# Layer 1 of a two-layer conv and scan kernel: another order of the steps, and y taken from PSUM by VectorE with xs times D in the same instruction

## The reference

```
x     = silu(depthwise_conv_5x5(x) + conv_b);  xs = x.reshape(B, C, L)
x_dbl = einsum('kd,bdl->bkl', x_proj_w, xs);   dts, Bs, Cs = x_dbl[:, :R], x_dbl[:, R:R+N], x_dbl[:, R+N:]
delta = softplus(einsum('dr,brl->bdl', dt_w, dts) + dt_b)
log_dA = maximum(delta * A, log(EPS));  P = exp(cumsum(log_dA, -1))
hs    = P * cumsum(delta * Bs * xs / maximum(P, EPS), -1)
y     = einsum('bdnl,bnl->bdl', hs, Cs) + xs * Ds
```

## Time and profile before

| | us |
|---|---|
| three runs | 4332.36, 4338.97, 4346.80; median 4338.97 |
| the profiled execution | 4340.87, of which the span in the trace is 4339.1 |
| layer 1 begins | about 1987 |
| one group inside the loop, from gate to gate | about 300 |
| the last group | about 249 |

### The profile page before, as it was taken

The page is one execution under the profiler, slowest core; times in us unless marked ns, Lnnn a source line. Parts: engine busy times, 40 slices in busy tenths (PEclk is TensorE's granted clock), DMA queues, the critical chain, the costliest instruction groups (busy, mean ns, idle before and its releaser), DMA issues.

```text
span 4339.1 us, 74865 instructions
## 1 busy us (share of the span) xinstructions
PE 3840.0 (88%) x22806; PEld 2793.4 (64%) x22806; DVE 3258.9 (75%) x5219; ACT 2790.3 (64%) x4796; POOL 2263.5 (52%) x1928
## 2 busy tenths in 40 slices
PE   6999999999999999887888889888888888898877
PEld 6787878888787878675555545545545555455432
DVE  3767666676767675605988978879879889789899
ACT  1545455454636363657887877878778778778775
POOL 0323223232323242405776867767768677677787
PEclk9999999999999999987997988979979979889877
DMA  7565555556464644373423324424324334243100
GB/s 233 146 186 150 174 161 160 174 147 183 135 196 124 212 123 142 80 184 82 109 71 92 103 57 106 115 51 109 98 61 108 79 81 109 61 108 92 37 20 22
DMA packets 314879, 507.44 MB, mean 117 GB/s; under 512 B 190000, under 2 KB 255248, under 8 KB 314144
## 3 DMA queue, kind: packets, MB, share of 16 engines
q1 hardware_dynamic: 314432, 502.08, 42.3%
HBM read 424.94 MB, written 77.07 MB: 116 GB/s over the span
## 4 chain that ended last, share of the span: by engine, by line
PE 22%; DVE 12%; issue 9%; ACT 7%; POOL 5%; DMA 1%; DVEq 1%; ACTq 0%; POOLq 0%; SPq 0%
PE ps_front L1313 6%; PE ps_y L1386 5%; DVE ps_q L1080 5%; DVE h L1107 5%; PE ps_front L1306 3%; PE ps_prep L1335 2%; POOL u L1000 2%; PE ps_y L1383 2%; POOL h L1011 2%; PE ps_front L1326 1%; PE ps_bc L1356 1%; ACT d_a L1201 1%; DMA out_dram<-y 1%; ACT d_a L1195 1%; ACT y L1221 1%
## 5 line engine op out<-in xcount | busy, mean ns | idle before, releaser
L1011 POOL TENSOR_TENSOR h<-h,c_rows 128x448 f32<-128x448 f32 x672 | 766.7, 1141 | 366.1 <-DVE ps_q L1114 194.6
L522 ACT ACTIVATE act_h<-ps_up,b 128x448 f32<-128x448 f32 x672 | 408.9, 635 | 778.5 <-PE ps_up L640 778.3
L1000 POOL TENSOR_TENSOR u<-dxs,b_rows 128x448 f32<-128x448 f32 x672 | 767.0, 1141 | 48.0 <-ACT b_rows L1209 42.3
L1386 PE MATMUL ps_y<-h,ident 128*128 128x448 f32 x1344 | 733.2, 633 | 35.0 <-POOL h L1011 25.4
L319 POOL TENSOR_TENSOR h_low<-act_h,h_high 128x448 fp32r<-128x448 f32 x224 | 287.7, 1284 | 900.6 <-ACT h_high L527 900.6
L1080 DVE TENSOR_TENSOR_SCAN ps_q<-d_a,q_last,ps_q 128x448 f32<-128x448 f32 x576 | 659.6, 1145 | 13.2 <-ACT d_a L1201 13.2
L1107 DVE TENSOR_TENSOR_SCAN h<-d_a,ps_q 128x448 f32<-128x448 f32 x576 | 648.3, 1126 | 6.5 <-issue 6.2
L1313 PEld LDWEIGHTS ps_front<-win,taps 120*112 120x112 f32 x4608 | 538.4, 188 | 139.8 <-issue 136.4
L613 PE MATMUL ps_stage<-win,taps 124*112 124x112 f32 x6144 | 607.2, 260 | 2.7 <-DVE w_low L366 2.7
L613 PEld LDWEIGHTS ps_stage<-win,taps 124*112 124x112 f32 x6144 | 607.0, 178 | 3.3 <-DVE w_low L366 2.8
L1313 PE MATMUL ps_front<-win,taps 120*112 120x112 f32 x4608 | 550.8, 273 | 7.5 <-ACT win L1151 3.7
(11 more groups left out here) (93 smaller groups left out, 7156.2 us busy)
## 6 DMA issues: line engine op xcount, KB each, us to landing
taps<-in_t_dram SPq DMA_DIRECT2D x192, 896.0 KB, 4.9
taps<-in_t_dram SPq DMA_DIRECT2D x192, 672.0 KB, 4.9
xres<-in_x_dram SPq DMA_DIRECT2D x224, 168.0 KB, 2.5
x_dram<-x1o SPq DMA_DIRECT2D x224, 168.0 KB, 2.0
x1pad<-x_dram SPq DMA_DIRECT2D x96, 392.0 KB, 8.1
out_dram<-y SPq DMA_DIRECT2D x168, 224.0 KB
xpad<-in_x_dram SPq DMA_DIRECT2D x29, 1176.0 KB, 10.4
conv<-in_x_dram SPq DMA_DIRECT2D x3, 1176.0 KB, 14.9
```

The source lines that it names most:

```text
L522: nc.scalar.activation(act_h[u % 2][:, t, :], ps_up[t][:, 0:BT], ACT.Gelu, bias=b1[:, t:t + 1]).then_inc(gelu_done, 1)
L1000: nc.gpsimd.tensor_tensor(u[s % U_SLOTS][:, :], dxs[:, t, :], b_rows[n][:, :], ALU.mult).then_inc(u_done, 1)
L1011: nc.gpsimd.tensor_tensor(h[s % H_SLOTS][:, :], h[s % H_SLOTS][:, :], c_rows[n][:, :], ALU.mult).then_inc(hc_done, 1)
L1386: nc.tensor.matmul(ps_y[:, 0:BT], ident[:, :], h[s % H_SLOTS][:, :], start=False, stop=(n == N - 1)).then_inc(y_added, 1)
```

## The change

1. `skip` and its product are gone. The first `add_y` of a run starts the accumulation.
2. `keep_y` moves from ScalarE to VectorE: one instruction reads `ps_y`, adds `xs` times `ds_col`, and writes `y`. It stands in the step in which TensorE's last add of the run stands (s = 5, 9, ... in place of ScalarE's 6, 10, ...), right behind `gate`. The last run of a group is taken in step 1 of the next. `silus` now waits for `y_kept`, since VectorE reads `xs` so late.
3. The tables change: `DELTA_AT = (4, 5, 8)`, `Z_AT = (5, 6, 9)`, `SUM_AT = (8, 9)` with the third tile at j = 0 of the band itself, `DXS_AT = (9, 11)` with the third at j = 1.
4. The front begins a step later, ends two steps earlier (three convs of the last block have both halves in one step), and the bursts stand at s = 0 (6 pieces), 41 (3), 63 (7) and 70 (5).
5. Within a step TensorE now does the pieces of the next band ahead of the front piece; ScalarE does the late softplus ahead of `keep_b`, and most front pieces at the step's end.
6. VectorE's first group is written out ahead of the loop, which now has six turns on that engine.

```diff
-        DELTA_AT = (3, 5, 7)
-        Z_AT = (4, 6, 8)
-        SUM_AT = (7, 9, 11)
-        DXS_AT = (8, 10, 11)
+        DELTA_AT = (4, 5, 8)
+        Z_AT = (5, 6, 9)
+        SUM_AT, LAST_SUM_AT = (8, 9), 0
+        DXS_AT, LAST_DXS_AT = (9, 11), 1
...
+            def keep_y(g, r):
+                b, t = r // TILES, r % TILES
+                dve.wait_ge(y_added, g * S + (r + 1) * N + H_SLOTS)
+                dve.wait_ge(y_stored, (g * RUNS + r + 1) * 16)
+                nc.vector.scalar_tensor_tensor(y[:, :], xs[:, t, b * BT:(b + 1) * BT], ds_col[:, t:t + 1],
+                                               ps_y[:, 0:BT], ALU.mult, ALU.add).then_inc(y_kept, 1)
...
                     gate(g, s)
+                    if s > N and (s - N - 1) % N == 0:
+                        keep_y(g, (s - N - 1) // N)
+                    if s == 1 and not first:
+                        keep_y(g - 1, RUNS - 1)
+                    if j == LAST_SUM_AT:
+                        sum_delta(g, b, TILES - 1)
                     if (more or b + 1 < BANDS) and j in SUM_AT:
                         sum_delta(f, fb, SUM_AT.index(j))
...
+                    act.wait_ge(y_kept, (f - 1) * RUNS + b * TILES + t + 1 + Y_BASE)
                     nc.scalar.activation(xs[:, t, b * BT:(b + 1) * BT], bank[i][:, 0:BT], ACT.Silu,
                                          bias=conv_bias[:, t:t + 1]).then_inc(front_kept, 1)
...
                 if n == 0:
-                    pe.wait_ge(y_kept, g * RUNS + r + 1)
-                    nc.tensor.matmul(ps_y[:, 0:BT], skip[:, t, :], xs[:, t, b * BT:(b + 1) * BT],
-                                     start=True, stop=False)
+                    pe.wait_ge(y_kept, g * RUNS + r + Y_BASE)
                 pe.wait_ge(hc_done, g * S + s + 1 + N)
                 nc.tensor.matmul(ps_y[:, 0:BT], ident[:, :], h[s % H_SLOTS][:, :],
-                                 start=False, stop=(n == N - 1)).then_inc(y_added, 1)
+                                 start=(n == 0), stop=(n == N - 1)).then_inc(y_added, 1)
```

More of the change, by code:

```diff
@@ L815, in layer1 @@
         KEPT = (BANDS - 1) * STEPS
+        Y_BASE = RUNS + 1
         CONVS = CB // CQ
@@ L822, in layer1, with place @@
         units, schedule, backs = [], [[] for _ in range(S)], [[] for _ in range(S)]
-        def place(step, unit):
-            for piece in range(HALVES if unit[0] == "conv" else 1):
-                schedule[step + piece].append((len(units), piece))
+        def place(step, unit, at_once=False):
+            i, count = len(units), HALVES if unit[0] == "conv" else 1
             units.append(unit)
+            for piece in range(count):
+                schedule[step].append((i, piece))
+                if piece + 1 == count or not at_once:
+                    step += 1
+            return step
         def place_backs(step, runs):
@@ L1129, in group @@
                     scan_h(g, s)
-            for t in range(TILES):
+            for t in range(TILES - 1):
                 sum_delta(0, 0, t, True)
-            if last:
-                with dve.Fori(0, last) as g:
-                    group(g, True)
+            assert last > 1
+            group(0, True, True)
+            with dve.Fori(1, last) as g:
+                group(g, True)
             group(last, False)
+            keep_y(last, RUNS - 1)
         @block.scalar
@@ L1392, in group @@
                     f, fb = next_band(g, b)
[L1393 to L1397 removed]
+                    prepare = more or b + 1 < BANDS
+                    burst = backs[s] if more or s == 0 else ()
+                    starts = [i for i, piece in schedule[s] if piece == 0] if more else ()
+                    early = [i for i in starts if units[i][0] == "turn"] if not burst else ()
+                    for i in early:
+                        front_waits(g + 1, i)
                     if s >= Y_LAG:
                         add_y(g, s - Y_LAG)
[L1400 removed]
+                    if burst and starts:
                         for i in burst:
[L1402 to L1403 removed]
+                            back(g + 1, i)
+                    for i in starts:
+                        if i not in early:
                             front_waits(g + 1, i)
@@ L1406, in group @@
                         spread_c(g, b, SPREAD_C_NOW[j])
+                    for t in range(TILES):
+                        if prepare and j == PROJECT_AT[t]:
+                            project(f, fb, t)
+                    if prepare and j in DELTA_AT:
+                        delta_rows(f, fb, DELTA_AT.index(j))
+                    if prepare and j in SPREAD_B_AT:
+                        spread_b(f, fb, SPREAD_B_AT.index(j))
+                    if prepare and j in SPREAD_C_AT:
+                        spread_c(f, fb, SPREAD_C_AT.index(j))
+                    if burst and not starts:
+                        for i in burst:
+                            back(g if s == 0 else g + 1, i)
                     if more:
```

103 lines of the change are left out of this document (40 added, 63 removed).

## The result

| | before | changed |
|---|---|---|
| median of the runs | 4342.08 us | 4984.73 us |
| lowest and highest | 4332.36, 4346.8 | 4980.59, 4989.76 |
| profiled execution, its span | 4339.1 us | 4988.0 us |

The ratio is 1.1484, with a 95% interval of 1.146 to 1.1508: 643 us slower. The forecast was slower too, but 4690 us, and even its upper end, 4868, was too low.

A forecast was written before the change was run, and what follows sets the result against it. VectorE was taken as the bound. To 4340.9 us were added 91 (instruction), 212 (j = 9), 61 (j = 1), 163 (bursts), -284 (old waits), 113 (clock) and -4 (small things), +352: 4690 us, own range 4490 to 4870, chance 0.75.

The forecast's parts named there:

- the first row of VectorE's waits: Sign on VectorE: a new first row, y waiting for TensorE's add, 168 instances, about 4 us in every band at j = 9.
- VectorE's instruction: On VectorE: 168 new y instructions at 0.54 us each on its path, +91 us (91 to 109).
- The waits of before: VectorE's old waits, for softplus, `u` and smaller things, all go: -284 us (bounds 200 and 284).
- j = 9: VectorE's y at band step 9 waits for TensorE's last add: 4.3 us in 42 bands, 2.2 in 14, +212 us.
- j = 1: VectorE's y at band step 1 waits 1.7 us for TensorE in five bands of seven groups: +61 us.
- The ring: Steps j = 7 to 9: VectorE's `delta`, ScalarE's clip and `b_rows`, TensorE's spread to last add, VectorE's y; 7.2 us against 2.85.
- The bursts: At steps 63, 70 and 0, y waits behind TensorE's bursts: 22.5 us in seven groups, 5 in the last, +163 us.
- The store: At step 63's burst, the store, which had made a copy wait 1.91 us there, was counted in y's 9 us wait.
- The clock: TensorE's clock falls during waits: 1.7 us in 42 rings, 6 us at seven group starts, +113 us (0 to 290).
- A: Rival: only VectorE's list counts, old waits stay about as they are, 4341 + 91 = 4432 us; chance 0.12.
- C: Rival: TensorE, relieved of 390 us, stays ahead and each last add ends before gate plus 0.54; 4228 us; chance 0.09.

The follow-up runs named there:

- store_early: The changed kernel with SyncE's store of y ahead of the loads of its step and two steps earlier: 4888.42 us.
- late3_store: The changed kernel with y two steps later on VectorE and SyncE's store ahead of the loads, ScalarE's list unchanged: 4365.48 us.
- y_alone: The kernel before in its order, with y on VectorE, no diagonal product or copy, and three back pieces moved to the next group's first step: 4709.48 us.
- The halves: Against the kernel before: the changed order with y made the old way, 4365.78 us; the old order with y on VectorE, 4709.48 us.

## Why the prediction was half right

The sign, the first row of VectorE's waits and the mechanism were right; the size was not. Point by point, by its own terms:

*VectorE's instruction*, +91: it was 99. It is 0.678 us long, not 0.61, and 0.59 on the path.

*The waits of before*, -284: right to a few us. Softplus has vanished from the rows and `u` is down to 2.2.

The waits in front of y were forecast as 212 + 61 + 163 + 113 = 549, and were 844. With the clock's shares put where the prediction had them, and the waits summed up from the timeline over all eight groups:

| the y of | forecast | measured |
|---|---|---|
| j = 9, 42 bands with front work | 181 + 71 = 252 | 313.3 |
| j = 9, 14 bands without | 31 | 62.7 |
| j = 1, five bands of seven groups | 61 | 168.0 |
| s = 5, 65 and 73 of seven groups | 157 + 42 = 200 | 271.4 |
| elsewhere in the last group | 5 | 22.4 |
| elsewhere | 0 | 6.3 |

The 295 us of difference are the whole error (4985 - 4690).

*j = 9.* The ring was right, link by link, and opening it gave 198 us. Where nothing else came in, the size was right too: 4.3 + 1.7 = 6.0 us forecast, 5.9 and 6.3 at s = 21 and 33. That is partly luck, since the 1.7 was no more than a third of a bound. The rest has other causes: TensorE comes late out of the burst at s = 45 (8.7), the store holds y at s = 57 (9.0), and at s = 9 (7.5) and 69 (7.2) more of the ring runs at the low clock. The 14 bands without front work were given no clock at all; at s = 81 both adds of the ring take 1.86 us. There y waits 5.0 us, and 4.6 in the last group, not 2.2.

*j = 1* is the largest miss, and here the step failed: it was counted at full clock, and the clock term had nothing for it. Measured were 2.9 to 5.1 us, and 8.6 at s = 61, where the store adds to it, in place of 1.75. At s = 25 VectorE was ready 13.4 us behind the y of j = 9, as counted (13.3), but TensorE's last add ended at 18.4 and not at 15.0: the wait at j = 9 had come back to TensorE as a wait of 2.67 us, and behind it the turn, the add and the projections ran at the low clock (1.71, 1.86 and 3.35 us, where the count had 1.8 for the projections).

*The bursts*, 22.5 us a group and 6 for the clock: the y of s = 5, 65 and 73 waited 15.6, 13.6 and 9.0 us, 38.2 together, where I had 6.5, 9 and 7. At s = 65 it is the store; without it (store_early) 7.4. The largest miss is s = 5. TensorE there, in the fourth group, whose first gate is at 3146.1:
```profile
3162.97 1.70 PE L1322 MATMUL ps_front<-ident,x1pad 32*120 32x32 f32 x15
3164.60 1.86 PE L1400 MATMUL ps_y<-h,ident 128*128 128x448 f32 x2
...
3175.63 1.86 PE L1400 MATMUL ps_y<-h,ident 128*128 128x448 f32 x2
```
VectorE wants y at 16 us, as counted, but the last add, the one at 3175.63, ends at 31.4 us and not at 23. A turn and an add at the low clock take 3.4 us (1.70 and 1.86, a little overlapped), more than VectorE's step of 2.92, so TensorE catches up on nothing until the clock rises. Of these 9 us the clock term held 6.

*The store.* The prediction had it in one step, at some 2 us. It waits in three, 31 us a group and 218 in all, because SyncE's list puts loads that wait for TensorE ahead of it. This was written in the order and I read only VectorE's, ScalarE's and TensorE's lists. With the store ahead of the loads and two steps earlier, 96 us came back.

*The clock*, +113 with a range of 0 to 290: right in kind, too small in size and put in too few places (the rings with front work and the starts of the groups). Filling one gap gives 83 us back; what the low clock costs in all was not measured. From step 12 to step 35 of a group, without a burst, the granted clock fell from 0.98 to 0.81, as forecast.

So the step that failed is the clock term, with the count of j = 1 that it should have held, and beside it the store's place, at some 2 us. Of the rivals, A is the one to note: its number, 4432 us, missed by 550, but with enough slack (late3_store, 4365 us) its idea holds, that VectorE's own list decides. The section "Identifying the Most-Contended Engine" of the Trainium skill's "Perfetto Trace Analysis", by which A was argued, looks at occupancy (the 4432 came from the rows, the page states no number); here the waits of one instruction decided, on an engine that was busy for 67% of the span. C would have needed TensorE's last add ahead of the gate; y_alone shows 132 waits for it even in the old order.

The error in the reasoning, not in a number, is that the terms were added. The halves cost 25 and 369 us, and both together 643. A wait of VectorE delays ScalarE's clip and that TensorE's spread; TensorE then runs at its lower clock, and the next y waits again. The rows from step 21 to step 25 show this once, link by link; that the other bands go the same way is read from their waits only. TensorE's front pieces come later with it, and so do the loads that SyncE holds for them. A sum of separate terms has no place for this, and its high end should have been wider.

## What to carry to other kernels

Before an engine is given a result that another produces, look for how late the producer runs there, and put the reader that many steps behind. One step later, a change of one number, gave back 411 of 643 us, and two steps with an early store 619. Read every queue's list for what stands ahead of the release of the buffer, the store's queue among them. Ask of every engine whether its clock is the full one in the stretch that is counted. And test the order of two instructions in the kernel in which it will stand: the same swap gave 198 us in one kernel and cost 195 in another.

## What the runs showed of the hardware that was not expected

- An engine with less to do was busy for longer. TensorE lost 336 matmuls and its busy time rose from 3840.0 to 4130.4 us, since the same 12 matmuls take 1.43 us at a granted clock of 1.00 and 2.58 us at 0.50, behind a wait of 6.45 us.
- Work that nobody needs can pay. 1344 repeated matmuls in TensorE's gap made the kernel 83 us faster (4984.73 to 4901.95). Repeats at two more steps, where there was no gap, took 60 of them back (4962.43).
- VectorE's `y`, one operand in PSUM and a scalar from a column, takes 678 ns for 128 x 448 elements, where the gate takes 629 and `delta` 615.
